# First attention: in the steps that carry PV, the scores of both parts back to back, and both PV pieces between the two groups of transposes

## What is computed

```python
x = x + _L0_attn_ref(_layernorm(x, axis=-1), ...)
# inside, H = 16 heads, D = 64, per batch element b and head h:
Q1, Q2 = (Q[..., :d], Q[..., d:])        # the two "parts"
K1, K2 = (K[..., :d], K[..., d:])
A1 = jnp.einsum('bhqd,bhkd->bhqk', Q1, K1) * s
A2 = jnp.einsum('bhqd,bhkd->bhqk', Q2, K2) * s
P = jax.nn.softmax(A1, axis=-1) - lam * jax.nn.softmax(A2, axis=-1)
O = jnp.einsum('bhqk,bhkd->bhqd', P, V)
Y = Ocat @ Wo + bo                       # then a layer norm of Y, times 0.2
```

## Time and profile before

| | |
|---|---|
| median of 3 runs | 1793.45 us (1793.15 to 1796.05) |
| the profiled execution | 1794.79 us, its span 1793.0 us |
| TensorE's mean granted clock | 0.951 |
| busy share of the span | PE 89%, DVE 75%, ACT 71%, POOL 54% |
| one iteration of the first attention | 36.19 us |

### The profile page before, as it was taken

How to read it: one execution, slowest core, us unless ns; L and a number is a source line. 1 busy time by engine, 2 the same in 40 slices (tenths; PEclk the granted TensorE clock), 3 DMA queues, 4 the chain that set the end, 5 groups by cost and what they waited for, 6 DMA issues and landing times.

```text
span 1793.0 us, 28055 instructions
## 1 busy us (share of the span) xinstructions
PE 1598.6 (89%) x10499; PEld 636.6 (36%) x10499; DVE 1341.1 (75%) x2027; ACT 1274.5 (71%) x2062; POOL 960.1 (54%) x658
## 2 busy tenths in 40 slices
PE   5999999999999999999999999975777999999853
PEld 2444333433343333333343334324621222222212
DVE  5777777777777777777777777769589888888418
ACT  4877787778778777877787877854253877777841
POOL 2898777777777777777777777840000001111110
PEclk9999999999999999999999999997686999999976
DMA  4100011011111110101010110000010000000000
GB/s 122 23 22 21 24 35 24 20 27 32 25 22 26 27 30 21 24 22 38 21 24 24 32 24 20 23 8 1 1 42 1 14 14 14 14 14 14 14 14 24
DMA packets 50433, 42.34 MB, mean 24 GB/s; under 512 B 26021, under 2 KB 39242, under 8 KB 50298
## 3 DMA queue, kind: packets, MB, share of 16 engines
q1 hardware_dynamic: 50298, 40.55, 9.4%
HBM read 20.27 MB, written 1.31 MB: 12 GB/s over the span
## 4 chain that ended last, share of the span: by engine, by line
PE 55%; DVE 21%; issue 14%; ACT 7%; POOL 1%; DMA 1%; SPq 0%; ACTq 0%; POOLq 0%; DVEq 0%
PE PS L1420 14%; PE PS L1396 12%; PE PS L1408 11%; DVE nmx L1011 8%; PE PS L1742 4%; PE PS L1444 4%; ACT ering L734 3%; DVE mxp L1286 2%; PE PS L1463 2%; PE PS L1709 2%; DVE on L1041 2%; DVE yT L1053 2%; PE PS L1726 2%; PE PS L1684 1%; ACT ering L910 1%
## 5 line engine op out<-in xcount | busy, mean ns | idle before, releaser
L1011 DVE TENSOR_REDUCE nmx<-PS 128x1 f32<-128x1024 f32 x512 | 625.6, 1222 | 248.8 <-PE PS L1397 248.4
L557 POOL TENSOR_TENSOR ering<-ering 128x1024 f32<-128x1024 f32 x256 | 603.5, 2357 | 21.4
L734 ACT ACTIVATE ering<-PS,nmx 128x1024 f32<-128x1024 f32 x512 | 571.3, 1116 | 40.7 <-DVE nmx L1011 40.4
L1396 PE MATMUL PS<-region 64*128 64x512 f16 x1536 | 420.3, 381 | 18.1 <-ACT ering L734 13.7
L555 POOL TENSOR_SCALAR ering<-ering,rho 128x1024 f32<-128x1024 f32 x256 | 286.5, 1119 | 252.6 <-DVE rho L1020 251.7
L1397 PE MATMUL PS<-region 64*128 64x512 f16 x1536 | 420.3, 381 | 0.0
L1408 PE MATMUL PS<-ident,ering 128*128 128x128 f32 x2048 | 334.5, 286 | 15.6 <-ACT t L745 7.4
L1286 DVE TENSOR_REDUCE mxp<-PS 128x2 f32<-128x1024 f32 x256 | 303.4, 1219 | 45.5 <-PE PS L1726 39.7
L1408 PEld LDWEIGHTS PS<-ident,ering 128*128 128x128 f32 x2048 | 217.6, 141 | 295.2 <-issue 98.4
L910 ACT ACTIVATE ering<-PS 128x1024 f32<-128x1024 f32 x256 | 258.3, 1024 | 89.6 <-PE PS L1709 82.3
L1396 PEld LDWEIGHTS PS<-region 64*128 64x128 f16 x1536 | 104.9, 94 | 286.8 <-ACT ering L734 171.7
(11 more groups left out here) (287 smaller groups left out, 1863.5 us busy)
## 6 DMA issues: line engine op xcount, KB each, us to landing
region<-region SPq DMA_DIRECT2D x64, 256.0 KB, 3.6
osb<-scr SPq DMA_DIRECT2D x32, 128.0 KB, 3.3
rcp<-scr SPq DMA_DIRECT2D x32, 128.0 KB, 3.3
rcp<-scr SPq DMA_DIRECT2D x64, 64.0 KB, 2.0
x<-in_L_attn_X SPq DMA_DIRECT2D x4, 256.0 KB, 3.3
wq_raw<-in_L_attn_Wq SPq DMA_DIRECT2D x16, 64.0 KB, 3.2
wk_s<-in_L_attn_Wk SPq DMA_DIRECT2D x16, 64.0 KB, 1.9
wo_s<-in_L_attn_Wo SPq DMA_DIRECT2D x32, 32.0 KB, 2.6
```

What stands on the lines that cost most here:

```text
L557: P.tensor_tensor(e1, e1, e2, ALU.subtract).then_inc(s_sub_ok, 1)
L734: A.activation((E1, E2)[p][s % 4], PS[:, bank:bank + 2, :].rearrange("p a b -> p (a b)"), ACT.Exp, bias=nmx[:, 2 * s + p:2 * s + p + 1], s ...
L1011: V.tensor_reduce(nmx[:, 2 * s + p:2 * s + p + 1], PS[:, bank:bank + 2, :].rearrange("p a b -> p (a b)"), AX.X, ALU.max, negate=True).then ...
L1396: MM(PS[:, bank, :], top[0:64, ql, q], KT[b][0:64, p, kl, :], start=(j == 0), stop=(j == 2))
```

## The change

In steps 3 to 6 of iterations 1 to 31 (those with PV of the iteration before and scores of their own) the PE's list was A, PV, T0, B, T1, PV. It becomes A, B, T0, PV, PV, T1. The other steps, and the four steps with PV after the last iteration, keep their order, and no other engine's list changes. No wait is added or dropped, but the waits that stood ahead of the first PV piece in step 3 now stand ahead of B(3).

```diff
@@ -1521,10 +1521,16 @@
                                 pe.wait_ge(s_b1_ev, 1)
                             if nxt:
                                 pe.wait_ge(s_klo_ok, 2 * (n + 2))
-                        values(n - 1, 2 * s - 6)
+                        if not own:
+                            values(n - 1, 2 * s - 6)
+                    if own and 3 <= s < 7 and prv:
+                        scores(n, s, 1)
                     if later:
                         turn(m, (s + 5) % 8, 0)
-                    if own:
+                    if 3 <= s < 7 and prv and own:
+                        values(n - 1, 2 * s - 6)
+                        values(n - 1, 2 * s - 5)
+                    if own and not (3 <= s < 7 and prv):
                         scores(n, s, 1)
                     if later:
                         turn(m, (s + 5) % 8, 1)
@@ -1536,7 +1542,7 @@
                         turn_w(2 * s - 4)
                     if s == 6 and n == 0:
                         project_v(1)
-                    if 3 <= s < 7 and prv:
+                    if 3 <= s < 7 and prv and not own:
                         values(n - 1, 2 * s - 5)
                     if s == 7 and 0 <= n <= last0 - 3:
                         project_v(n + 2)
```

## The result

| | before | after |
|---|---|---|
| median of 4 runs | 1794.75 us (1793.15 to 1796.49) | 1832.39 us (1827.85 to 1835.04) |
| ratio | | 1.0207, 95% interval 1.0182 to 1.0232 |
| profiled execution, its span | 1794.79, 1793.0 | 1827.85, 1826.1 |
| one iteration of the first attention | 36.19 | 37.15, and 38.6 to 38.7 in six |

The change makes the kernel 2.1% slower. It was forecast slower, at 1822.0 with 1806 to 1838 around it; the time lies 10 us above the forecast.

The account below looks back on a forecast made before the run. PE was taken to bound the kernel. Per iteration +1.45 - 0.66 + 0.24 = +1.03 us, 29 times +29.9, less 1.3 for two other iterations: +28.6 on 1793.45 gives 1822.0 us, range 1806 to 1838.

Parts of the forecast that it names:

- A to B in a row: Steps 3 to 6 on PE: the boundary between adjacent score groups costs 0.22 us instead of 0.31, a gain of 0.09.
- PV pieces in a row: Steps 3 to 6 on PE: two adjacent PV pieces take 1.87 us, gaining 0.15 (between 0 and 0.15).
- a step with PV: A reordered step on PE without a stall: 4.48 us against 4.70, a gain of 0.22, bounds 0.09 and 0.25.
- A(3) to B(3): Step 3 on PE: B(3) still starts 2.35 us after A(3), since it waits for `low_q`.
- PE stands still there: Step 3, ahead of B(3): PE could start it 0.67 us after A(3), so it stands still for 1.68.
- A(3) to A(4): Length of step 3 on PE: 6.15 us against 4.70, a loss of 1.45.
- steps 4 to 6: These steps on PE take 4.48 us against 4.70 or 4.71: -0.22 each, -0.66 in all, no new wait costed.
- way out of step 6: T1 ending step 6 delays step 7's T1 to 2.34 us after A(7), from 2.10: +0.24, bounds 0 and 0.35.
- falls of the clock: Rival: each of 29 stalls in step 3 also lowers PE's clock, +46 us more, or 1868; chance 0.04.
- rival of slack that takes up the stall: PE's waits in step 1 (0.37 us) and at A(3) (0.44) shorten, absorbing part of the loss: 1798.5; chance 0.07.
- second rival: Wait at B(3) not binding or repaid elsewhere, only fewer switches count: faster, 1766 to 1774 us; chance 0.04.
- Iteration 3: A(3) comes late with `low_q` done, so no stall; with iteration 31, -1.3 us for the two.

Follow-up runs that it names:

- the last version: Kernel before with step 3 as A, PV, PV, T0, B, T1; steps 4 and 5 in the new order; step 6 as A, B, T0, PV, T1, PV: 1772.2 us.

## Why the prediction was right, point by point

| term | predicted | measured |
|---|---|---|
| A to B in a row | gain 0.09 | 0.10 (0.21 for 0.31) |
| PV pieces in a row | gain 0.15 | 0.15 (1.87 to T1) |
| a step with PV | 4.48 | 4.44 |
| A(3) to B(3) | 2.35 | 2.41 |
| PE stands still there | 1.68 of distance | 1.74 of distance (2.41 - 0.67); the row's bracket says 1.59, 29 times |
| A(3) to A(4) | 6.15 (+1.45) | 6.20 (+1.50) |
| steps 4 to 6 | -0.66 | -0.79 |
| way out of step 6, A(7) to T1 | 2.34 (+0.24) | 2.34 (+0.24) |
| an iteration | 37.2 (+1.03) | 37.15 (+0.96) |
| falls of the clock | none (rival: 29, +1.59 each) | 6 in the profile, +1.54 each |

**The step that carried the result** was to ask, for the group that moves forward, what releases it, and not only what PE does meanwhile. `low_q` ended 0.09 us ahead of a B(3) that looked as if it had never waited. The row that gave it away was the count of 29 with hardly any microseconds behind it. That step 3 turns the gain into a loss is shown by dividing the change: old order in step 3, -0.54; new order in step 3 alone, +1.50. That it does so by the wait is shown by the version in which both PV pieces stand ahead of B(3): nobody waits for `low_q`, and an iteration takes 35.50.

**The gain was costed a little low.** A step takes 4.44, not 4.48, since I rounded the distances up. That is 0.13 an iteration for three steps, and the hand-over after the standing still took back 0.06 (2.41 for 2.35).

**That steps 4 to 6 meet no new wait** held: they are dense, at 4.44 each. The way out of step 6 was right in size and in mechanism.

**What failed was the weight of the clock.** The prediction put the clock forward as a rival that either does not happen or happens at each of the 29 stalls, gave it 0.04, and named a fall of the clock in step 3 as a sign of being wrong. That sign came, in six iterations. The price of one fall was about right (1.59, measured 1.54). The argument against it was one row, a gap of 1.64 us in iteration 0 after which the clock stayed up; one gap without a fall does not show that 29 others will have none. The change does not touch that place, and in two of the ten profiles the clock did fall behind the same gap: in the version with the old step 3 and in the last version. Iteration 0 took 38.04 us in both, where the kernel before has 37.19. This is the version with the old step 3: the transposes behind the gap take 0.78 instead of 0.66, and the mean clock of the 2.23 us from their start is 0.59, where it is 1.00 in the kernel before.

```profile
39.97 0.78 PE L1363 MATMUL PS<-ident,region 128*128 128x128 f32 x4 [1.64 <-ACT small L713]
```

```profile
39.97:42.20 2.23, 2.23 (x12) 1.51 (x14) 1.16 (x3) 0.56 (x2) 0.94 (x1) 0.59 0.62 129
```

The falls are most of what lies between 1822.0 and 1832.4. The two versions whose idle time was filled, and which have the same iteration of 37.15, took 1821.6 and 1821.7, 26 us over the kernel before against the 28.6 of the sum. That the time still lay in the range is luck in this term: nothing in the working said six falls, and 29 of them at 1.54 would have added 45 us and led far past 1838. By the Trainium skill (TensorE: Matmul & The Clock Gate, section What's actually happening) activity lifts a clock that is low by default; the falls behind the stall, and their absence once the gap is filled, agree with it.

**The rival of slack that takes up the stall** is refuted: filled or not, an iteration stays 0.96 longer, and A(3) still waits 0.44 us for its exponential.

**The second rival** had only the fewer switches count. With fewer switches between unlike groups and the wait avoided, the kernel runs at 1772, close to its 1774. The Trainium skill's rule on draining (TensorEngine Tiling (Array Packing), section Key Properties) agrees with that part: a boundary between unlike shapes costs 0.10 to 0.15 us here, and that cost is gone between like ones. That draining is where the time goes is not shown.

**Iteration 3** was predicted to gain 0.6. From its `low_q` to the next it took 40.88 before and 38.58 in the changed kernel's profile, but 40.0, 41.6 and 41.6 in the three other profiles whose normal iteration is 37.15. It differs from execution to execution, and carries no conclusion.

## What to carry to other kernels

A group that never seems to wait may be ready only just in time: before work is taken from in front of it, subtract its releaser's end from its start. Two like groups in a row on PE saved 0.10 to 0.15 us here for each boundary between unlike shapes that went away, so a new order should be built from like groups, with each group that has a late input behind enough other work. Where a stall on PE of some 1.6 us repeats, look at the granted clock behind it, iteration by iteration.

## What the runs showed of the hardware

The boundary between groups of unlike tile shapes costs PE 0.10 us (scores to something else) to 0.15 us (PV: entry and exit), and nothing of that is left between two groups of the same shape. After 1.59 us of standing still the granted clock fell in 6, 6 and 5 of 29 iterations in three profiles, and cost some 1.5 to 1.6 us each time (once, in iteration 1, it could not be told from another loss); with 0.94 and 0.30 us left of it, the rest filled with matmuls, in none of 29. After a gap of 1.64 us in iteration 0 it fell in two of ten profiles. The same useless matmuls that stopped the falls cost no time, since they ran inside the wait.
